# Two-layer cross-attention kernel: the parts of the score maxima and the row normalizations move from VectorE to GpSimd, and the key loads from ScalarE's queue to SyncE's

## The chip, the cores and the metric

One core of one Trainium2 chip. The metric is the device time of one execution in microseconds. The kernel before takes 761.01 us, the median of 3 runs (759.99 to 761.21).

## The reference

`x` is 16 batches of 112 rows of 256 features; the context is 16 batches of 375 rows of 256. Two layers follow each other.

```
x = x + xattn0(layernorm(x), ctx, ctx, mask)      # one head, masked, with a norm of its output
x = x + ffn0(layernorm(x))                        # mixture of experts: 8 routed (2 used per row), 2 shared
x = x + xattn1(layernorm(x), ctx, ctx)            # 16 heads of 16 features, no mask
x = x + ffn1(layernorm(x))                        # x @ W.T + b + (x @ V_r) @ C.T

xattn1: q, k, v = heads of queries @ Wq.T, keys @ Wk.T, values @ Wv.T
        attn = softmax(q @ k.T / sqrt(16)) ; out = (attn @ v) @ Wo.T
layernorm(x) = (x - mean) / sqrt(var + 1e-5)
```

Everything is in float32. The change touches the third line and the normalizations ahead of the third and fourth.

## The kernel before

The first layer and the experts take the time up to about 540 us. The second layer's loop runs over the batches b = 0 to 14, with the two batches ahead begun before it and the last batch behind it (`tensor`, `vector`, `scalar`, `gpsimd` and `sync` of `second_layer` each hold their own copy of that order). All orders are written out by hand, and engines meet only at semaphores. Four batches are a group i (b // 4).

**Scores twice.** The softmax needs the maximum of each row of scores. TensorE multiplies queries and keys once for the maxima (`scores(b, g)`, two heads at a time, g = 0 to 7, line 2134), and VectorE reads the two banks (`maximum(b, g)`, line 1769). The exponentials need the scores the other way round, keys on the partitions, with the maximum taken off. For this queries and keys have rows of their own under the real ones: bf16 parts of a float32 value in three rows each (96 rows are real, `DEPTH`), then three rows that hold the maximum split into three bf16 parts on the queries' side (`qst`), and a constant under the keys (`kst`). `transposed(b, q, ks)` (line 2154) multiplies all 128 rows, so that the maximum is subtracted inside the product. ScalarE takes the exponential (`exps`, line 1981), and TensorE multiplies by the values (`outputs(b, q)`, line 2163), turns the outputs (`outputs_T`, line 2172), and VectorE divides by the sums (`finish(b)`, lines 1794 and 1796, "the heads").

**How the maxima get there.** After `maximum(b, 7)`, `negated_parts(b)` splits the maxima in four small VectorE steps (lines 1776 to 1782). TensorE turns the 48 columns over (`maxima_T(b)`, line 2139), VectorE copies them (`turned(b)`, line 1788), and SyncE sends them as three small transfers to the three rows under the queries (`maxima(b)`, line 1620, "the rows of maxima"). TensorE waits for them ahead of `transposed(b, 0)`.

**The batches overlap.** In iteration b, TensorE makes the scores of batch b + 2, turns the maxima of b + 1, and does the exponentials' products and the outputs of b. Scores use two pairs of banks in turn (`PAIR`, `EARLIER`): a product may start when the one before it in that pair was read. The turned outputs, and the blocks below, take places in that same sequence.

**Blocks.** Between them lie pieces of other stages for a group of four batches: `("q", 3)` in b = 5 (queries of the last group), `("o", i)` in b = 6, 10 and 13 (output projection and addition, `attended`), `("f", i)` in b = 8, 12 and in the tail (the last linear layer, `results`). Each needs normalized rows, apart from "o": `NORMALIZED` puts the statistics (`mean_var`, lines 1719 to 1726) and the normalization (`normalized`, line 1732) of "q" 3 in b = 4 and of "f" 0, 1 and 2 in b = 7, 11 and 14, both on VectorE. GpSimd makes the reciprocal root between them (`rstd_of`, lines 1657 and 1659), adds the last bias (`add_bias`, line 1653), gathers the experts' rows of the last group (`gather`, line 1668), sums them (`combine`, line 1691), and splits queries into bf16 parts (`split_queries`, `split_rest`, lines 1595 to 1603).

**Loads.** The keys of batch b + 4 (three transfers of 378 KB, `load_keys`, line 1571) are asked for on ScalarE's queue at the end of iteration b, after its last exponential. The values of batch b + 1 go the same way for b up to 8 (408 KB). The split queries of a group are stored and loaded again on ScalarE's queue (`store_queries`, `load_queries`).

Of the kernel before, what the change touches and what calls it, by code (L numbers as in the profile page):

```python
# [15 lines left out]
P = 128  # L16
B, S, D = 16, 112, 256
K = 375
# [21 lines left out]
TWO_ONES = 1.0 + 0x3F80 / 2.0 ** 23  # L40
# [1429 lines left out]
def second_layer(nc, tensors, first, routed, dram, out, x_res, weight1, weight2, slots, mhalf, ps, bank, ident, new_semaphore, pool_semaphore):  # L1470
# [111 lines left out]
    def ones_below(pool, b):  # L1582
        pool.memset(kst[b][DEPTH:P, :, :].rearrange("p h t -> p (h t)").bitcast(F32), TWO_ONES).then_inc(s["ones_ready"], 1)
        pool.wait_ge(s["ones_ready"], b + 1)
# [14 lines left out]
    def split_rest(eng, i):  # L1599
        eng.wait_ge(s["q2_ready"], 3 * i + 2)  # L1600
        eng.tensor_copy(qa[:, 2, :, :], qr[:]).then_inc(s["q2_ready"], 1)
        eng.wait_ge(s["q2_ready"], 3 * i + 3)
        eng.tensor_tensor(qa[:, 0, :, :], qr[:], qa[:, 2, :, :], ALU.subtract).then_inc(s["q3_ready"], 1)
        eng.wait_ge(s["q3_ready"], i + 1)

# [4 lines left out]
    def sync(sp):  # L1610
        def load_values(b):
            sp.dma_start(vt[:, b % 2, :, :, :].rearrange("p c h d -> p (c h d)"), vscr[b]).then_inc(s[f"v_in{b % 2}"], 16)

        def maxima(b):
            i, j = divmod(b, G)
            sp.wait_ge(s["mT_ready"], b + 1)

            sp.wait_ge(s["below_ready"], min(i, 1) + 1)
            for k in range(3):
                sp.dma_start(qst[i % 2][DEPTH + k:DEPTH + k + 1, :, j * S:(j + 1) * S], mT[k * NH:(k + 1) * NH, b % 2, :]).then_inc(s[f"mrow_in{b % 2}"], 16)  # L1620

        def results(i):
            for j in range(G):
                sp.wait_ge(s["res_ready"], i * G + (j + 1))
                sp.dma_start(out[i * G + j], x_res[:, i * G + j, :]).then_inc(s["res_out"], 16)


        sp.wait_ge(routed["w2_ready"], NTILE)
        load_keys(sp, 1)
        load_context(sp, NV + 1)  # L1630
        load_context(sp, NV + 2)
        load_values(0)
        for b in range(NV, NV + 3):
            sp.wait_ge(s["v_ps"], b + 1)
            load_context(sp, b + 3)
        maxima(0)
        load_values(1)

        for b in range(B):
            if b + 1 < B:  # L1640
                maxima(b + 1)
            what, i = blocks_in(b)
            if what == "f":
                results(i)
        results(NG - 1)
        sp.wait_ge(s["res_out"], 16 * B)
# [8 lines left out]
    def rstd_of(pool, n, norm, js=slice(0, G)):  # L1655
# [3 lines left out]
        pool.tensor_tensor(rstd[:, js], rstd[:, js], mhalf[:, js], ALU.pow).then_inc(s["rstd_ready"], 1)  # L1659

# [22 lines left out]
    def gpsimd(pool, n):  # L1683

        def combine(i):
            for j in range(G):
# [16 lines left out]
        for j in range(G):  # L1703
            pool.wait_ge(s["p_ready"], (2 * j + 2) * NKC)
            gather(pool, i, j)
        combine(i)
        rstd_of(pool, n, NORMS["q", i])
        split_queries(pool, i)
        split_rest(pool, i)
        for i in range(NG - 1):  # L1710
            rstd_of(pool, n, NORMS["f", i])
            add_bias(pool, i)
# [4 lines left out]
    def mean_var(v, n, i, js=slice(0, G)):  # L1717
        for j in range(js.start, js.stop):
            v.bn_stats(stat[:, j, :], x_res[:, i * G + j, :]).then_inc(s["dve"], 1)
            n()  # L1720
        for j in range(js.start, js.stop):
# [41 lines left out]
    def vector(v, n):  # L1763
        V, done = nc.vector, s["dve"]

        def maximum(b, g):
            v.wait_ge(s["s_ps"], b * 8 + (g + 1))
            p = 2 * PAIR["score", b, g]
            V.tensor_reduce(mxh[:, 2 * g:2 * g + 2], ps[0:S, p:p + 2, 0:K], axis=AX_X, op=ALU.max).then_inc(s["s_max"], 1)  # L1769

        def negated_parts(b):
            base, slot = b * 4, b % 2
            v.wait_ge(s["s_max"], b * 8 + 8)
            if b >= 2:
                v.wait_ge(s["mT_ps"], b - 1)
            V.tensor_scalar(mparts[:, slot, 0, :], mxh[:], -1.0, None, ALU.mult).then_inc(s["m_ready"], 1)
            v.wait_ge(s["m_ready"], base + 1)
            V.scalar_tensor_tensor(mr[:, slot, :], mxh[:], -1.0, mparts[:, slot, 0, :], ALU.mult, ALU.subtract).then_inc(s["m_ready"], 1)
            v.wait_ge(s["m_ready"], base + 2)
            V.tensor_copy(mparts[:, slot, 1, :], mr[:, slot, :]).then_inc(s["m_ready"], 1)  # L1780
            v.wait_ge(s["m_ready"], base + 3)
            V.tensor_tensor(mparts[:, slot, 2, :], mr[:, slot, :], mparts[:, slot, 1, :], ALU.subtract).then_inc(s["m_ready"], 1)
# [50 lines left out]
        negated_parts(0)  # L1833
# [3 lines left out]
        negated_parts(1)  # L1837
# [4 lines left out]
        for b in range(B - 1):  # L1842
# [7 lines left out]
            if kind == "f":  # L1850
                v.wait_ge(s["x3_ready"], k * G + G)
                mean_var(v, n, k)
            elif kind == "q":
# [7 lines left out]
            if kind is not None:  # L1861
                normalized(v, k, NORMS[kind, k])
# [3 lines left out]
            if what == "o":  # L1866
                attended(i)
            elif what == "f":
                results(i)
            if ahead_of:  # L1870
                maximum(b + 2, 7)
                negated_parts(b + 2)
# [73 lines left out]
    def scalar(a):  # L1946
# [59 lines left out]
        for b in range(B - 1):  # L2006
# [7 lines left out]
            if b == G + 2:  # L2014
                store_queries(a, NG - 1)
# [17 lines left out]
            if b + 4 < B:  # L2033
                load_keys(a, b + 4)
# [322 lines left out]
def build_program(nc, dram, outs):  # L2357
    with ExitStack() as ctx, ExitStack() as semaphores:
# [30 lines left out]
        with ExitStack() as lent:  # L2389
# [5 lines left out]
                ("heads", [S, B, D], F32), ("xhL", [P, C, GS], F32), ("mxh", [S, NH], F32), ("mr", [S, 2, NH], F32),  # L2395
# [88 lines left out]
```

## Time and profile before

| | |
|---|---|
| median of 3 runs | 761.01 us |
| profiled execution: its own time | 762.61 us |
| its span | 760.8 us |
| TensorE busy | 732.4 us (96%) |
| VectorE busy | 479.4 us (63%) |
| ScalarE busy | 311.0 us (41%) |
| GpSimd busy | 243.0 us (32%) |
| granted TensorE clock, mean | 0.991 |

The busy shares are of the whole span. The span is the time from the first to the last instruction of the profiled execution; its own time is a little longer. In the rows of stretches, each row is a stretch from one turn of the maxima (line 2139) to the next, so b=3 is 593.75:602.89, b=4, 5, 6 and 7 follow it, and the last two are b=10 and b=11. In the rows, PE is TensorE's products, PEld its loading of weights, DVE VectorE, ACT ScalarE, POOL GpSimd, SP SyncE, and a trailing q is an engine's queue that issues transfers. "[0.94 <-DVE mxh L1769]" behind a row says that the engine was idle for 0.94 us before it, and what ended that.

### The profile page before, as it was taken

Reading aid. Unit: us, or ns where it says so; the run is one execution under the profiler, and the core shown is the slowest. Engines: PE = TensorE matmul, PEld = TensorE weight load, DVE = VectorE, ACT = ScalarE, POOL = GpSimd, SP = SyncE. Lnnn points to the kernel's source line nnn. Section 1 sums busy time; section 2 is a strip of 40 time slices with the busy share of each in tenths; the row PEclk is TensorE's granted clock in tenths of the full one; section 3 lists DMA queues with packets and bytes.
Section 4 is the critical chain, followed back from the end, with each engine's and each line's share of the span. In section 5 each row is a group of like instructions: output and inputs, shape, how many; then the busy total and the mean of one; then the engine's idle time right before and its main releaser. Section 6 shows DMA issues by size and latency. Waiting matters only on the chain.

```text
span 760.8 us, 15546 instructions
## 1 busy us (share of the span) xinstructions
PE 732.4 (96%) x5784; PEld 564.9 (74%) x5784; DVE 479.4 (63%) x1122; ACT 311.0 (41%) x556; POOL 243.0 (32%) x250
## 2 busy tenths in 40 slices
PE   7899999999999999999999999999999998999996
PEld 4576667776776676589999998989777766676775
DVE  4468665356727667824444564838678978888745
ACT  1223211241124122245554555554246764565561
POOL 3775712371151242601301414223743211102021
PEclk9998999999999999999999999999999999999999
DMA  9499932542250296912443423354987765654101
GB/s 257 120 273 326 261 115 83 184 143 82 81 165 13 66 368 249 315 42 69 124 130 102 132 66 99 119 148 125 252 225 207 203 160 170 171 137 125 28 3 49
DMA packets 73068, 113.87 MB, mean 150 GB/s; under 512 B 14929, under 2 KB 59346, under 8 KB 71074
## 3 DMA queue, kind: packets, MB, share of 16 engines
q1 hardware_dynamic: 59200, 66.24, 29.5%
q10 hardware_dynamic: 7634, 30.97, 14.9%
q0 software_dynamic: 6160, 15.67, 6.5%
q8 instruction: 47, 0.77, 0.4%
q14 instruction: 27, 0.22, 0.1%
HBM read 84.27 MB, written 28.41 MB: 148 GB/s over the span
## 4 chain that ended last, share of the span: by engine, by line
PE 79%; DVE 9%; DMA 5%; POOL 3%; issue 1%; ACT 1%; ACTq 0%; SPq 0%; DVEq 0%; POOLq 0%
PE ps L1439 16%; PE ps L1074 12%; PE ps L1448 8%; PE ps L1089 7%; DVE mxh L1769 4%; PE ps L1108 4%; PE ps L2134 4%; PE ps L2163 4%; DMA mask_i<-in_mask 3%; PE ps L2154 3%; PE ps L2127 2%; PE ps L1120 2%; PE ps L1044 2%; PE ps L1016 2%; PE ps L2108 2%; PE ps L2063 2%
## 5 line engine op out<-in xcount | busy, mean ns | idle before, releaser
L1439 PE MATMUL ps<-rowsT,w 128*128 128x128 f32 x1120 | 130.8, 275 | 0.0
L1439 PEld LDWEIGHTS ps<-rowsT,w 128*128 128x128 f32 x1120 | 128.0, 192 | 0.1
L1769 DVE TENSOR_REDUCE mxh<-ps 112x2 f32<-112x750 f32 x128 | 115.0, 931 | 20.1 <-PE ps L2134 18.7
L1981 ACT ACTIVATE d_pT<-ps 125x448 f32<-125x448 f32 x192 | 92.8, 548 | 67.0 <-PE ps L2154 63.5
L1074 PE MATMUL ps<-x1T,sw 128*128 128x448 f32 x256 | 101.3, 540 | 0.0
L1393 ACT ACTIVATE w<-rw 128x1024 f32 x70 | 73.8, 1056 | 59.4 <-PE ps L1439 57.0
L1074 PEld LDWEIGHTS ps<-x1T,sw 128*128 128x128 f32 x256 | 47.5, 190 | 38.8 <-issue 35.9
L2134 PE MATMUL ps<-kst,qst 96*112 96x375 bf16 x256 | 63.8, 336 | 5.9 <-DVE mxh L1769 3.0
L1332 POOL DMA_DIRECT2D yscr<-y x35 | 19.7, 562 | 154.1 <-DVE y L1366 154.1
L1448 PE MATMUL ps<-rw,h 128*128 x280 | 66.4, 380 | 0.0
L884 ACT ACTIVATE silu<-ps,sb 128x448 f32<-128x448 f32 x32 | 20.3, 635 | 98.4 <-PE ps L1074 98.4
L1089 PE MATMUL ps<-sw,gluT 128*112 128x256 f32 x256 | 57.8, 379 | 0.0
L2154 PE MATMUL ps<-qst,kst 128*128 128x112 bf16 x768 | 55.4, 213 | 0.8 <-DMA qst<-mT 0.5
L1448 PEld LDWEIGHTS ps<-rw,h 128*128 128x128 f32 x280 | 50.7, 190 | 6.8 <-issue 1.4
L2154 PEld LDWEIGHTS ps<-qst,kst 128*128 128x128 bf16 x768 | 47.0, 98 | 11.4 <-DMA qst<-mT 1.1
L1089 PEld LDWEIGHTS ps<-sw,gluT 128*112 128x112 f32 x256 | 44.8, 177 | 10.5 <-issue 0.4
L1351 DVE TENSOR_TENSOR h<-ps,rb 128x512 f32<-128x512 f32 x35 | 24.1, 689 | 37.6 <-PE ps L1439 37.6
L341 POOL DMA_INDIRECT xg<-xh_moe,places x32 | 32.5, 1016 | 46.7 <-PE ps L1074 21.9
L1355 DVE TENSOR_TENSOR h<-ps,rb 128x512 f32<-128x512 f32 x35 | 24.2, 691 | 32.5 <-PE ps L1439 32.5
L1668 POOL DMA_INDIRECT yg<-yscr,slots x32 | 31.1, 971 | 25.3 <-ACT d_pT L1981 16.8
L500 DVE SCALAR_TENSOR_TENSOR gluT<-ps,sb,silu 128x448 f32<-128x448 f32 x32 | 21.8, 681 | 26.9 <-ACT silu L884 26.5
L2134 PEld LDWEIGHTS ps<-kst,qst 96*112 96x112 bf16 x256 | 24.2, 129 | 19.6 <-issue 9.4
(248 smaller groups left out, 1188.2 us busy)
## 6 DMA issues: line engine op xcount, KB each, us to landing
kst<-kscr ACTq DMA_DIRECT2D x45, 378.0 KB, 5.2
rw<-in_rw SPq DMA_DIRECT2D x24, 512.0 KB, 9.9
kscr<-ka SPq DMA_DIRECT2D x16, 567.0 KB, 4.1
cT<-in_ctx_t SPq DMA_DIRECT2D x17, 378.0 KB, 5.0
ctxT<-in_ctx_t SPq DMA_DIRECT2D x16, 378.0 KB
ctxn<-in_ctx SPq DMA_DIRECT2D x16, 336.0 KB
qst<-qscr ACTq DMA_DIRECT2D x12, 448.0 KB, 6.5
rows<-xg SPq DMA_DIRECT2D x35, 128.0 KB, 2.7
```

The costliest lines, as they stand in the source:

```text
L341: pool.indirect_dma_start(out=dram["xg"], out_offset=bass.IndirectOffsetOnAxis(ap=places[0:S, k, b:b + 1], axis=0), in_=xh_moe[:, b, :], i ...
L1074: last = mm(bank[up_in(i, m)[k]][:, 0:GS], (sw1, sw2)[k][:, e, c, h * P:(h + 1) * P], x1T[:, c, :], start=c == 0, stop=c == C - 1)
L1089: last = mm(bank[down_in(i, j)][0:S, 0:D], gluT[:, m, j * S:(j + 1) * S], sw3[:, e, h, :], start=m == 0, stop=m == U - 1)
L1108: last = mm(ps[:, 2 + m, 0:KP], wk1[:, c, m * P:(m + 1) * P], context_T(b)[:, c, :], start=c == 0, stop=c == C - 1)
L1393: A(w12[:, k, :, :], (rw1, rw2)[k][:, e, :, :], ACT.Copy).then_inc(s[("w1_ready", "w2_ready")[k]], 1)
L1439: last = mm(bank[1 + 2 * q + k][:, block], w12[:, k, c, block], rowsT[:, q, c * P:(c + 1) * P], start=c == 0, stop=c == C - 1)
L1448: last = mm(y_bank(n)[:, 0:D], h2[:, q, m * P:(m + 1) * P], rw3[:, e, m, :], start=m == 0, stop=m == HM - 1)
L1668: pool.indirect_dma_start(out=yg[:, j, k, :], out_offset=None, in_=yscr[0:DONE[i] * P, :], in_offset=bass.IndirectOffsetOnAxis(ap=slots[0: ...
L1769: V.tensor_reduce(mxh[:, 2 * g:2 * g + 2], ps[0:S, p:p + 2, 0:K], axis=AX_X, op=ALU.max).then_inc(s["s_max"], 1)
L1981: A(pT[:, q % 2, k, :], bank[4 + k][0:KC, 0:QUAD * S], ACT.Exp).then_inc(s["p_ready"], 1)
L2134: last = mm(pair_bank(("score", b, g), k)[0:S, 0:K], qst[i % 2][0:DEPTH, h, j * S:(j + 1) * S], kst[b % 4][0:DEPTH, h, 0:K], start=True, s ...
L2154: last = mm(bank[4 + k][:, h * S:(h + 1) * S], kst[b % 4][:, QUAD * q + h, k * KC:k * KC + P], qst[i % 2][:, QUAD * q + h, j * S:(j + 1) * ...
```

## The change

VectorE's `negated_parts` becomes `parted`, and for batches 2 to 15 GpSimd runs it; the parts are now of the maximum itself and the constant under the keys is minus one instead of one. The maxima have two slots, so that the maxima of one batch can be read while those of the next are written. `normalized_beside` lets GpSimd normalize the rows of "q" 3 and of "f" 0, 1 and 2. VectorE makes the statistics of "f" in the "o" block itself (b = 6, 10, 13): two rows' between the additions, the others after maximum 7. The statistics of "q" 3 stay in b = 4. SyncE asks for the keys of batch b + 4, after the rows of maxima of b + 1 and a wait for the last product of `transposed(b, 3)`. `store_queries` of the last group moves from the start of b = 6 to its end.

```diff
-TWO_ONES = 1.0 + 0x3F80 / 2.0 ** 23
+TWO_MINUS_ONES = -1.0 - 0xBF80 / 2.0 ** 23
...
+    def parted(eng, b):
+        base, slot = b * 4, b % 2
+        eng.wait_ge(s["s_max"], b * 8 + 8)
+        if b >= 2:
+            eng.wait_ge(s["mT_ps"], b - 1)
+        eng.tensor_copy(mparts[:, slot, 0, :], mxh[:, slot, :]).then_inc(s["m_ready"], 1)
+        eng.wait_ge(s["m_ready"], base + 1)
+        eng.tensor_tensor(mr[:, slot, :], mxh[:, slot, :], mparts[:, slot, 0, :], ALU.subtract).then_inc(s["m_ready"], 1)
+        eng.wait_ge(s["m_ready"], base + 2)
+        eng.tensor_copy(mparts[:, slot, 1, :], mr[:, slot, :]).then_inc(s["m_ready"], 1)
+        eng.wait_ge(s["m_ready"], base + 3)
+        eng.tensor_tensor(mparts[:, slot, 2, :], mr[:, slot, :], mparts[:, slot, 1, :], ALU.subtract).then_inc(s["m_ready"], 1)
...
     # sync, loop over b
             if what == "f":
                 results(i)
+            if b + 4 < B:
+                sp.wait_ge(s["st_ps"], (b + 1) * 4 * NKC)
+                load_keys(sp, b + 4)
...
+    def normalized_beside(pool, i, norm):
+        pool.wait_ge(s["rstd_ready"], MV + norm + 1)
+        for j in range(G):
+            pool.tensor_scalar(xh[:, j, :], x_res[:, i * G + j, :], mv[:, j, 0:1], rstd[:, j:j + 1],
+                               ALU.subtract, ALU.mult).then_inc(s["xh_ready"], 1)
...
     # gpsimd
         for j in range(G):
+            if j % 2:
+                parted(pool, j // 2 + 2)
             pool.wait_ge(s["p_ready"], (2 * j + 2) * NKC)
             gather(pool, i, j)
-        combine(i)
+        for j in range(0, G, 2):
+            combine(i, range(j, j + 2))
+            parted(pool, j // 2 + 4)
         rstd_of(pool, n, NORMS["q", i])
+        normalized_beside(pool, i, NORMS["q", i])
+        parted(pool, 6)
+        parted(pool, 7)
         split_queries(pool, i)
         split_rest(pool, i)
-        for i in range(NG - 1):
+        for i, batches in enumerate(((8,), (9, 10, 11, 12), (13, 14, 15))):
+            for b in batches:
+                parted(pool, b)
             rstd_of(pool, n, NORMS["f", i])
+            normalized_beside(pool, i, NORMS["f", i])
             add_bias(pool, i)
...
     # vector
         def maximum(b, g):
+            if g == 0 and b >= 2:
+                v.wait_ge(s["m_ready"], (b - 2) * 4 + 2)
...
     # vector, loop over b
             turned(b + 1)
-            if kind == "f":
-                v.wait_ge(s["x3_ready"], k * G + G)
-                mean_var(v, n, k)
-            elif kind == "q":
+            if kind == "q":
                 v.wait_ge(s["added"], 2 * G)
                 mean_var(v, n, k)
             if b:
                 finish(b - 1)
...
-            if kind is not None:
-                normalized(v, k, NORMS[kind, k])
...
             if what == "o":
-                attended(i)
+                attended(i, slice(0, 2))
+                v.wait_ge(s["x3_ready"], i * G + 2)
+                row_stats(v, n, i, slice(0, 2))
+                attended(i, slice(2, G))
             elif what == "f":
                 results(i)
             if ahead_of:
                 maximum(b + 2, 7)
-                negated_parts(b + 2)
+            if what == "o":
+                v.wait_ge(s["x3_ready"], i * G + G)
+                row_stats(v, n, i, slice(2, G))
+                rows_joined(v, n)
...
     # scalar, loop over b
             exps(b, 0, range(2, NKC))
-            if b == G + 2:
-                store_queries(a, NG - 1)
             exps(b, 1)
...
             exps(b, 3, range(1, NKC))
-            if b + 4 < B:
-                load_keys(a, b + 4)
+            if b == G + 2:
+                store_queries(a, NG - 1)
```

## Rows read from the trace of the kernel before

**Rows 1.** Busy by stretch: us, PE, PEld, DVE, ACT, POOL, clock, DMA share, GB/s.
```profile
593.75:602.89 9.14, 9.14 (x167) 6.77 (x165) 8.49 (x16) 7.63 (x18) 2.92 (x4) 1.00 0.68 182
602.89:614.15 11.26, 9.54 (x167) 6.76 (x165) 11.09 (x28) 6.17 (x14) 1.28 (x2) 1.00 1.02 258
614.15:628.40 14.25, 13.21 (x183) 9.07 (x182) 9.81 (x15) 8.34 (x18) 3.87 (x4) 1.00 0.53 135
628.40:642.89 14.49, 13.82 (x189) 10.38 (x189) 11.09 (x21) 6.82 (x15) 1.80 (x1) 1.00 0.47 144
642.89:654.39 11.50, 9.53 (x168) 6.84 (x166) 11.18 (x28) 6.18 (x14) 4.05 (x6) 1.00 0.60 167
...
677.52:691.21 13.69, 13.57 (x191) 10.36 (x189) 10.09 (x20) 7.14 (x16) 0.00 (x0) 1.00 0.33 86
691.21:702.46 11.25, 9.52 (x167) 6.85 (x166) 11.08 (x28) 6.18 (x14) 4.04 (x6) 1.00 0.51 128
```

**Rows 2.** Waits from 550 us on: total us, times, longest.
```profile
ACT d_pT L1981 <- POOL qa L1603: 3.0, 1, 3.0
PE ps L2134 <- DVE mxh L1769: 3.0, 4, 0.9
PE ps L2134 <- DVE heads L1796: 2.6, 3, 1.0
PEld ps L2154 <- DMA qst<-mT: 1.1, 2, 0.9
```

**Rows 3.** Timeline of b=7, VectorE and TensorE: start, duration, instruction.
```profile
643.62 1.41 DVE L1719 BATCH_NORM_STATS2 d_stat<-x_res 112x6 f32<-112x256 f32 x4 [0.15 <-issue]
...
645.96 0.53 PE L2134 MATMUL ps<-kst,qst 96*112 96x375 bf16 x2 [1.04 <-DVE heads L1796]
...
648.36 1.37 DVE L1732 TENSOR_SCALAR d_xh<-x_res,d_mv,d_rstd 112x256 f32<-112x256 f32 x4
...
650.63 0.53 PE L2134 MATMUL ps<-kst,qst 96*112 96x375 bf16 x2 [0.94 <-DVE mxh L1769]
```

**Rows 4.** Timeline of the end of b=5.
```profile
625.31 1.89 POOL L1597 TENSOR_TENSOR qr<-qr,qa 128x896 f32<-128x896 f32 x1
625.39 1.84 DVE L1778 SCALAR_TENSOR_TENSOR mr<-mxh,mparts 112x16 f32<-112x16 f32 x1
...
627.26 0.17 DVE L1780 CAST mparts<-mr 112x16 bf16<-112x16 f32 x1
...
628.40 0.21 PE L2139 MATMUL ps<-identb,mparts 112*48 112x112 bf16 x1 [0.93 <-DVE mparts L1782]
```

**Rows 5.** Timeline of a plain stretch, b=2 to b=3.
```profile
589.85 1.77 DVE L1769 TENSOR_REDUCE mxh<-ps 112x2 f32<-112x750 f32 x2
...
592.84 0.34 ACTq L1988 DMA_DIRECT2D vt<-vscr  x1
...
593.75 0.23 PE L2139 MATMUL ps<-identb,mparts 112*48 112x112 bf16 x1
...
594.34 2.74 SPq L1620 DMA_DIRECT2D qst<-mT  x3
...
600.50 0.55 PEld L2154 LDWEIGHTS ps<-qst,kst 128*128 128x128 bf16 x8
```

**Rows 6.** Groups of GpSimd's instructions by line: busy us, mean ns.
```profile
L296 POOL TENSOR_SCALAR keep<-mask_i 112x375 f32<-112x375 int32 x16 | 24.6, 1538 | 28.0 <-DVE nmx L443 17.7 <-DMA mask_i<-in_mask 10.1
...
L1657 POOL TENSOR_SCALAR d_rstd<-d_mv 112x4 f32<-112x4 f32 x7 | 1.6, 231 | 93.6 <-DVE d_mv L1726 93.6
...
L1659 POOL TENSOR_TENSOR d_rstd<-d_rstd,mhalf 112x1 f32<-112x1 f32 x1 | 0.6, 567 | 0.1
```

**Rows 7.** Transfers from 560 us on: KB each, median us to landing.
```profile
kst<-kscr ACTq DMA_DIRECT2D x38, 378.0 KB, 5.2
vt<-vscr ACTq DMA_DIRECT2D x8, 408.0 KB, 6.1
```

**Rows 8.** Landing of the rows of maxima, whole second layer.
```profile
DMA to landing us min/median/max: 1.7/3.8/7.6
```

More of the change, by code:

```diff
@@ L1582, in ones_below @@
     def ones_below(pool, b):
-        pool.memset(kst[b][DEPTH:P, :, :].rearrange("p h t -> p (h t)").bitcast(F32), TWO_ONES).then_inc(s["ones_ready"], 1)
+        pool.memset(kst[b][DEPTH:P, :, :].rearrange("p h t -> p (h t)").bitcast(F32), TWO_MINUS_ONES).then_inc(s["ones_ready"], 1)
         pool.wait_ge(s["ones_ready"], b + 1)
@@ L1683, in gpsimd, with combine @@
     def gpsimd(pool, n):
-        def combine(i):
-            for j in range(G):
+        def combine(i, js):
+            for j in js:
                 for k in range(2):
@@ L1715, in gpsimd, with row_stats @@
         rstd_of(pool, n, NORMS["f", i] + 1, LAST)
-    def mean_var(v, n, i, js=slice(0, G)):
+    def row_stats(v, n, i, js=slice(0, G)):
         for j in range(js.start, js.stop):
@@ L1720, in mean_var, with rows_joined @@
             n()
+    def mean_var(v, n, i, js=slice(0, G)):
+        row_stats(v, n, i, js)
+        rows_joined(v, n, js)
+    def rows_joined(v, n, js=slice(0, G)):
         for j in range(js.start, js.stop):
@@ L1766, in maximum @@
         def maximum(b, g):
+            if g == 0 and b >= 2:
+                v.wait_ge(s["m_ready"], (b - 2) * 4 + 2)
             v.wait_ge(s["s_ps"], b * 8 + (g + 1))
             p = 2 * PAIR["score", b, g]
[L1769 to L1782, printed above, removed]
+            V.tensor_reduce(mxh[:, b % 2, 2 * g:2 * g + 2], ps[0:S, p:p + 2, 0:K], axis=AX_X, op=ALU.max).then_inc(s["s_max"], 1)
         def turned(b):
@@ L1832, in vector @@
             maximum(0, g)
-        negated_parts(0)
+        parted(v, 0)
         turned(0)
@@ L1836, in vector @@
             maximum(1, g)
-        negated_parts(1)
+        parted(v, 1)
         v.wait_ge(s["v_ready"], B)
@@ L2394, in build_program @@
                 ("d_pT", [KC, 2, NKC, GS], F32), ("outT", [P, 4, S], F32),
-                ("heads", [S, B, D], F32), ("xhL", [P, C, GS], F32), ("mxh", [S, NH], F32), ("mr", [S, 2, NH], F32),
+                ("heads", [S, B, D], F32), ("xhL", [P, C, GS], F32), ("mxh", [S, 2, NH], F32), ("mr", [S, 2, NH], F32),
                 ("mparts", [S, 2, 3, NH], BF16), ("mT", [3 * NH, 2, S], BF16), ("rec", [S, NH], F32)))
```

## The prediction, made before the change was run

> **What bounds the kernel now.** The change touches only the second layer's attention, from about 565 us on, so I read that part alone. I number the stretches by the loop's batch b, and cut them where TensorE turns the maxima of the next batch over. First view: busy time by stretch [rows 1]. A stretch with nothing but attention takes 9.14 us and TensorE is busy all of it (b=3: 9.14 of 9.14); one with a block ("q", "o" or "f") takes 13.69 us (b=10). Those two are TensorE's own pace, and nothing that the other engines save there can count. Four kinds of stretch stand above the pace: b=4 by 2.12 us (11.26), b=7 by 2.36 (11.50), b=11 by 2.11 (11.25), and b=5 and b=6, which I come back to. In b=4, 7 and 11 VectorE is busy for 11.1 to 11.2 us of 11.25 to 11.5, against 8.5 us in a plain stretch: these are the three batches in which it makes row statistics and normalizes rows while scores are still to be read.
>
> Second view: TensorE's waits [rows 2]. Scores wait 2.6 us three times for the heads and 3.0 us four times for maxima, all told. Third view: the order of time in b=7 [rows 3]. The statistics (1.41 us) stand ahead of the heads, and TensorE waits for these and starts score 3 after 1.04 us of idleness. The four normalizations (1.37 us) stand ahead of maximum 5, and TensorE idles another 0.94 us. So the price of rows work on VectorE is about 1 us for each of the two places, in each of three stretches. In b=14 the same work costs nothing: there are no more scores ahead, and the last 32 us (tail) go by exponentials and products.
>
> Fourth view: the end of b=5 [rows 4]. VectorE's second step of the parts took 1.84 us instead of 0.17, and ended with GpSimd's subtraction of the queries (625.31 + 1.89). TensorE then waited 0.93 us to turn the maxima over, and stretch b=6 is 14.49, 0.80 above its pace. That accident costs 0.93 + 0.80 = 1.73 us.
>
> **The change, part by part.**
>
> *Parts on GpSimd.* Four VectorE steps per batch go for batches 2 to 15, and GpSimd does them. Budget: in a plain stretch the last maximum ends at 589.85 + 1.77 = 591.62 and TensorE wants the parts at 593.75 [rows 5], so 2.13 us. GpSimd has no such instruction before the change. Nearest rows [rows 6]: a scalar operation on 4 columns 0.23 us, a power of one column 0.57. Lower bound for a step: VectorE's 0.17 us (the cast in [rows 4]); upper bound that 0.57. I take 0.25: these are 16 columns, nearest to the 4-column row. With about 0.1 us between steps (each waits for the one before) and at the ends the chain is 4 x 0.25 + 0.4 = 1.4 us: hidden by the score products and exponentials, with 0.7 us to spare. At 0.57 for the two subtractions and 0.3 for the two copies it is 2.1 us: just at the edge. Cost 0 in stretches; if the cover went, each 0.1 us beyond 2.13 would cost 0.1 us in each of 13 stretches. Only in b=13, where no scores stand between, is the gap shorter: 0 to 0.5 us late, I take 0.1.
>
> What stands in GpSimd's queue around it: parts of 2 and 3 stand ahead of two gathers, which then start about 1.7 us later. Their rows are scaled a batch later, so nobody waits. In b=2 and 3 the parts follow the sums of the gathered rows, whose last ends within 0.2 us of the last maximum. Parts of 7 now stand ahead of the query split and not beside it: the accident of b=5 and 6 goes, gain 1.7 us.
>
> In plain stretches VectorE gets back about 0.8 us, worth nothing: TensorE is already busy throughout.
>
> *Two slots of maxima.* The new wait of a batch's first maximum is for parts made a whole stretch earlier: 0.
>
> *Normalizing on GpSimd.* Nearest row: a two-operation scalar instruction on 375 columns, 1.54 us [rows 6]; by column this is 1.05 us for 256. Lower bound VectorE's 0.34 (1.37 / 4, [rows 3]), upper 1.54; I take 1.05, so 4.2 us for four. For "q" 3 they end near 611 and are wanted in b=5; for "f" 0 and 1 they start a stretch earlier than now and are wanted a stretch later. For "f" 2 they end about 735 where TensorE wants them about 736; at 1.54 each this would be 0.7 us late. So 0, and up to 0.7 for the range. It takes the normalizations out of VectorE in b=4, 7, 11: the second gap of each (0.94 us in b=7) goes.
>
> *Statistics moved to the "o" blocks (b=6, 10, 13).* Two of four go between the additions, while VectorE waits for products anyway (free). The other two and the joining (0.7 + 0.4 us) come after maximum 7, where the parts (0.8 us) have left. So VectorE enters b=7 and b=11 some 0.4 us later than now. Walking its queue: maximum 1 then ends about 0.2 us after TensorE wants that pair of banks; the heads end just in time. I take a new gap of 0.2 us (bounds 0 and 0.6). Net gain b=7: 2.36 - 0.2 = 2.15; b=11: 2.11 - 0.2 = 1.9. In b=13 it is beside TensorE's last score-free part: 0.
>
> *b=4.* Here ("q" 3) the statistics stay ahead of the heads, so the first gap of 1 us stays; only the second goes, at most 2.12 - 1.04 = 1.08 us. But TensorE met another wait right behind: about 0.2 us for the row of maxima (the shorter of two such waits, 1.1 us together and the longer, in b=1, 0.9 [rows 2]). Arriving 0.9 us earlier it finds the row 0.9 us farther away, unless it lands earlier. So the gain is 0 to 1.08; I take 0.7, as the row's landing moves a little with the earlier gathering of traffic.
>
> *Keys asked for by SyncE.* The request waits for the same product as the exponential that now stands ahead of it on ScalarE, so it starts at the same moment. ScalarE loses three issues (about 0.6 us each) per batch, in which its next exponential was not yet due: 0. But the transfers move to SyncE's queue, in front of the rows of maxima. Keys take 5.2 us to land, values 6.1 [rows 7], rows of maxima 3.8 in the median, 1.7 at best and 7.6 at worst [rows 8]. In a plain stretch values are asked for at 592.8 [rows 5] and all in flight has landed by 592.8 + 6.1 = 598.9; a row queued behind everything would then land some 1.7 us later, 600.6, and TensorE wants it at 600.5 [rows 5]. So even the full queue costs 0.1 us a stretch. I take 0.3 us over all for b=1, 2 and 9, bounds -0.5 and +2.
>
> The Trainium skill, "DMA: Bandwidth & Descriptors", section on queues, rings and completion order, says that an issuing engine has one ring on each DMA engine, consumed in order, and that a semaphore's increment lands only after every earlier write of that engine, across its queues. By the second half a row of maxima waits for the keys in either arrangement, and the move is worth 0; by the first half alone it would be the slower rival below. The 3.8 us in the median for so small a transfer, against 1.7 at best, agree with the second half.
>
> *The store of queries* moves from b=6's start to its end. ScalarE waited 3.0 us there for GpSimd [rows 2], which is part of the accident above; now the split ends near 632 and the store comes near 640: 0.
>
> *VectorE held up by GpSimd.* The stall in [rows 4] could return elsewhere, as GpSimd works more. What stays on VectorE in the loop reads either banks or one tile. The Trainium skill, "SBUF — State Buffer", on who interferes with whom, says that a VectorE instruction with two SBUF inputs is held by a GpSimd one that reads SBUF, one with a single input outside the two-port modes is not. The trace agrees: the 1.84 us step has two such inputs. By it the new order is free of the stall.
>
> Sum: 1.7 (b=5, 6) + 2.15 (b=7) + 1.9 (b=11) + 0.7 (b=4) - 0.1 (b=13) - 0.3 (rows of maxima) = 6.05 us. The profiled execution has a span of 760.8 us and took 762.61; the median is 761.01. I take the sum from the median: 755.0 us.
>
> **Rivals.**
> 1. *All stalls go.* The row of maxima lands early enough in b=4, and no new gap opens after "o": 1.7 + 2.36 + 2.11 + 1.08, and 0.5 us of the DMA wait in b=1: 7.8 us, 753.2; with b=4's first gap too, 752.2. For it: VectorE has 0.8 us more air everywhere. Against: b=4's statistics stay where they were.
> 2. *Half is given back.* Statistics after maximum 7 are late by 0.6 us in b=7 and 11, and b=4 gains nothing, f 2 comes 0.7 late, rows of maxima cost 1 us: 6.05 - 0.8 - 0.7 - 0.7 - 0.7 = 3.15, 757.9.
> 3. *Slower: rows of maxima behind keys.* If SyncE's queue delays each row by L, b=1 and b=4 lose all L (they wait already), and b=2, 3, 7 and 9 lose L less their slack (asked for at 594.3 and wanted at 600.5 [rows 5], 6.2 us, less 1.2 for three issues and 3.8 to land, so 1.2). It turns the gain at 2L + 4(L - 1.2) = 6, so L = 1.8 us; with L = 4 it loses 19.2, net 13 slower: 774. For it: DMA is busy up to all of the time in b=4 (share 1.02, [rows 1]). Against: the bound above, since the keys must land anyway.
> 4. *GpSimd's parts too slow.* Above 0.5 us a step the chain passes 2.13 us; at 1 us it takes 4.4 - 2.1 = 2.3 us in 13 stretches, 30 us: 785. Against: the power of one column, the slowest for its size, takes 0.57 [rows 6].
>
> **How the numbers follow.** Less than 0.2% (1.5 us) cannot be told from no change. Forecast 0.60 (own range 753 to 757.5), rival 1 0.12, rival 2 0.14, rival 3 0.11 (of which 0.06 within 0.2%, since an L near 1.8 just cancels), rival 4 0.03. Rivals 3 and 4 give slower 0.08 together; same 0.08, with a little of rival 2; faster 0.84. Range 752 to 759.5: it takes in rivals 1 and 2 and the bounds of the terms.
>
> **What would show it.** After: stretches like b=7 and b=11 near 9.3 us and b=4 near 10.4; b=5 and 6 without the wait for parts; GpSimd's four steps ending before the turn; steps of about 0.25 us, normalizations about 1.05; no row of maxima waited for by more than 1 us. Wrong if: TensorE waits for the row of maxima in most stretches, or for GpSimd's parts, or if plain stretches differ from 9.14 us, on which nothing here says that they can change.

## The result, and the profile after

The changed kernel takes 758.12 us (median of 12 runs, 754.61 to 761.41), the kernel before beside it 762.23 us (12 runs, 758.41 to 766.46). The ratio is 0.9926, 95% interval 0.9902 to 0.995; by it, from the 762.23, the gain is 5.6 us (interval 3.8 to 7.5); the two medians differ by 4.1. The forecast was 755.0 from 761.01, a ratio of 0.9921 and a gain of 6.05. A second series of 12 gave 757.74 us and a ratio of 0.9943 (0.9916 to 0.997), a gain of 4.3 (2.3 to 6.4). So both series show a gain, and its size is uncertain by some 2 us.

The profiled execution of after is a long one: span 759.6 us, own time 761.40. Its second layer begins late. The turn of the maxima in b=0 starts at 570.56 us, in the kernel before at 565.16, and in the other traces of this study anywhere from 561.09 to 571.81. That is ahead of everything that the change touches, so the spans say little here. I compare the 14 stretches from that turn to the turn of b=14: 164.00 us before, 157.40 after, 159.06 in a second trace of the changed kernel. Gains of 6.60 and 4.94 us, 5.8 in the mean. What follows b=14's turn is 31.64 us in both profiles.

Busy time by stretch of the changed kernel, same columns as [rows 1]; b=3, 4, 5, 6, 7, then b=10 and 11:

```profile
598.31:607.46 9.15, 9.15 (x167) 6.78 (x166) 7.93 (x12) 7.75 (x18) 3.69 (x8) 1.00 0.69 186
607.46:618.33 10.87, 9.52 (x168) 6.74 (x166) 9.31 (x20) 6.17 (x14) 6.91 (x10) 1.00 1.01 267
618.33:631.58 13.25, 13.13 (x183) 9.04 (x181) 8.12 (x12) 8.24 (x18) 1.88 (x6) 1.00 0.47 127
631.58:645.27 13.69, 13.57 (x192) 10.36 (x190) 10.98 (x24) 7.26 (x16) 6.21 (x9) 1.00 0.48 120
645.27:655.37 10.10, 9.32 (x168) 6.71 (x166) 7.98 (x12) 6.18 (x14) 8.77 (x13) 1.00 0.89 247
...
678.30:691.99 13.69, 13.57 (x192) 10.35 (x190) 10.98 (x24) 7.26 (x16) 1.74 (x6) 1.00 0.32 89
691.99:701.27 9.28, 9.22 (x168) 6.82 (x166) 8.11 (x12) 6.31 (x14) 8.72 (x13) 1.00 0.48 123
```

The plain stretch and the block are where they were (9.15, 13.69): TensorE's own pace. b=11 has come down to it, b=4 has hardly moved, b=7 has come a little more than halfway. b=6 lies on the pace of a block. b=5 is at 13.25, which every trace repeats that has neither the accident nor another load in this stretch, so the "q" block's own pace is 13.25 and not the 13.69 of the others. VectorE's 11.1 us of b=4, 7 and 11 are 9.3, 8.0 and 8.1.

The waits of the changed kernel from 550 us on, as in [rows 2]:

```profile
PEld ps L2183 <- DMA qst<-mT: 2.4, 4, 1.1
PE ps L2183 <- DMA qst<-mT: 1.3, 2, 0.8
PEld ps L2163 <- DVE heads L1826: 1.0, 1, 1.0
PE ps L2163 <- DVE heads L1826: 0.8, 1, 0.8
```

Products waited 5.6 us for VectorE's maxima and heads before [rows 2]; now it is 0.8, once, in b=4. In exchange they wait 1.3 us, in two waits, for the rows of maxima (before: 0.52 us once, in b=1). Both, in order of time (b=4, b=7):

```profile
616.08 0.57 PE L2183 MATMUL ps<-qst,kst 128*128 128x112 bf16 x8 [0.56 <-DMA qst<-mT]
653.12 0.57 PE L2183 MATMUL ps<-qst,kst 128*128 128x112 bf16 x8 [0.78 <-DMA qst<-mT]
```

GpSimd's new instructions, first the first two steps of the parts (counts, shortest/median/longest ns), then the timeline in b=13 and 14 with the normalizations:

```profile
L1612 POOL CAST mparts<-mxh x14: 190/196/197, 577.9 to 726.6; 112x16 bf16<-112x16 f32 x14
L1614 POOL TENSOR_TENSOR mr<-mxh,mparts x14: 217/218/223, 578.2 to 726.9; 112x16 f32<-112x16 f32 x14
```

```profile
726.58 0.20 POOL L1612 CAST mparts<-mxh 112x16 bf16<-112x16 f32 x1 [12.64 <-DVE mxh L1812]
...
727.41 0.22 POOL L1618 TENSOR_TENSOR mparts<-mr,mparts 112x16 bf16<-112x16 f32 x1
...
729.06 4.83 POOL L1683 TENSOR_SCALAR d_xh<-x_res,d_mv,d_rstd 112x256 f32<-112x256 f32 x4
```

A step takes 0.20 to 0.22 us (forecast 0.25) and the four 1.05 us from first start to last end (726.58 to 727.63, and the same to 0.02 elsewhere); four normalizations take 4.83 us (forecast 4.2), and end at 733.89, 1.20 us ahead of the first product that reads them (735.09). In b=2 the parts end at 597.32, 0.99 us ahead of the turn. The normalizations of "q" 3 end at 616.03 and not near 611 as forecast, and the parts of batch 6, which stand behind them, 1.28 us ahead of their turn. TensorE never waits for either.

### The profile page after: what moved, and what is told of

Same layout as the page of the kernel before. It is cut to its first block, busy times and chain, and to the rows that moved or that the text cites. A ratio compares the mean times of both kernels' runs of the same rounds, so it can differ in the third digit from the quotient of the medians.

```text
span 759.6 us, 15555 instructions
## 1 busy us (share of the span) xinstructions
PE 731.1 (96%) x5784; PEld 563.2 (74%) x5784; DVE 465.4 (61%) x1050; ACT 311.8 (41%) x556; POOL 273.6 (36%) x322
## 4 chain that ended last, share of the span: by engine, by line
PE 83%; DMA 7%; DVE 4%; SPq 3%; issue 1%; POOL 1%; ACT 1%; ACTq 0%; DVEq 0%; POOLq 0%
PE ps L1439 15%; PE ps L1074 12%; PE ps L1089 7%; PE ps L1448 7%; PE ps L2163 5%; PE ps L2192 5%; PE ps L1108 5%; PE ps L2183 4%; PE ps L1120 3%; PE ps L2156 2%; PE ps L1044 2%; PE ps L2137 2%; DMA mask_i<-in_mask 2%; PE ps L1051 2%; DMA qst<-mT 2%; PE ps L2092 2%
## 5 line engine op out<-in xcount | busy, mean ns | idle before, releaser
L1074 PE MATMUL ps<-x1T,sw 128*128 128x448 f32 x256 | 103.0, 547 | 0.0
```

The source lines that it names most:

```text
L1074: last = mm(bank[up_in(i, m)[k]][:, 0:GS], (sw1, sw2)[k][:, e, c, h * P:(h + 1) * P], x1T[:, c, :], start=c == 0, stop=c == C - 1)
```

## The experiments

All start from the changed kernel but one. "Stretch" is as above, the "sum" is that of the 14 stretches; each value is from one trace unless said. Experiments 1 to 8 and 11 have one run each, and its time says little: the turn in b=0, ahead of everything that was edited, is spread over 10.7 us.

| | sum of the 14 stretches, us | own time of the profiled run, us |
|---|---|---|
| before | 164.00 | 762.61 |
| changed, and once more (12) | 157.40, 159.06 | 761.40, 756.69 |
| 1 keys on ScalarE | 157.65 | 753.81 |
| 2 store in the middle | 156.74 | 762.00 |
| 3 store at the start | 162.79 | 761.98 |
| 4 statistics of "q" 3 early | 161.87 | 762.51 |
| 5 parts on VectorE | 162.66 | 759.17 |
| 6 normalizations on VectorE | 159.31 | 754.88 |
| 7 statistics of "f" ahead of the heads | 158.97 | 759.63 |
| 8 queries' load in b=5 | 156.92 | 751.45 |
| 9 both transfers moved | 157.29 | 756.67 |
| 10 the three moves | 155.53 | 755.73 |
| 11 kernel before, two orders | 162.60 | 760.89 |

The two traces of the changed kernel lie 1.66 us apart, so sums are told apart only beyond about that; single stretches without a transfer repeat to a few hundredths.

**1. Keys asked for by ScalarE again.**

```diff
-                sp.wait_ge(s["st_ps"], (b + 1) * 4 * NKC)
-                load_keys(sp, b + 4)
...
     # scalar, end of the loop, behind store_queries
+            if b + 4 < B:
+                load_keys(a, b + 4)
```

> The changed kernel, with the keys of batch b + 4 asked for on ScalarE's queue again; all else of the change stays. In the changed kernel TensorE waits for the row of maxima 0.78 us in b=7 (stretch 10.10 us) and 0.56 us in b=4 (10.87). Theory A (the rows of maxima now queue behind the keys on SyncE's queue): the wait in b=7 goes, the stretch falls to about 9.3 us, and rows of maxima land in 3.7 us or so as before, so this part of the change cost 0.8 us or more. Theory B (the cause is the store of the queries, 672 KB, now asked for at the end of b=6 and in flight in b=7; the queue of the keys does not matter): b=7 stays near 10.1 us and b=4 near 10.9.

```profile
599.79:610.85 11.06, 9.52 (x167) 6.74 (x166) 9.31 (x20) 6.17 (x14) 6.91 (x10) 1.00 1.02 264
610.85:624.10 13.25, 13.13 (x183) 9.05 (x181) 8.12 (x12) 8.07 (x18) 1.88 (x6) 1.00 0.48 126
624.10:638.65 14.55, 14.00 (x191) 10.39 (x189) 11.48 (x24) 6.98 (x16) 6.97 (x10) 1.00 0.52 150
638.65:647.80 9.15, 9.15 (x166) 6.78 (x166) 7.58 (x11) 6.17 (x14) 8.03 (x12) 1.00 0.73 194
```

b=4 to b=7. The wait in b=7 is gone, as A says, but b=6 has lost as much (14.55 against 13.69): ScalarE's queue now issues the store and three key loads one after the other, from 634.28 to 637.14, and its next exponential starts at 637.18 after 2.36 us of idleness; TensorE waits 0.31 us for it, and is busy for 14.00 us of the stretch instead of 13.57. In b=7 the rows of maxima land in 4.4 to 4.9 us (5.2 to 6.0 in the changed kernel), but the store is also asked for 4.9 us ahead of them instead of 4.1, so this run alone does not tell A from B. The sum, 157.65 us, lies between the two traces of the changed kernel. So the queue of the keys is worth nothing that these traces can tell, on this path; what it does is keep ScalarE's queue clear where the store stands.

**2. Store in the middle of b=6.**

```diff
             exps(b, 2, range(1, NKC))
+            if b == G + 2:
+                store_queries(a, NG - 1)
             scaled(b, 2)
...
             exps(b, 3, range(1, NKC))
-            if b == G + 2:
-                store_queries(a, NG - 1)
```

> The changed kernel, with the store of the last group's queries moved from the end of b=6 to its middle, behind the exponentials of the third quarter, some 5 us earlier. Theory A (queue of the keys): b=7 stays at about 10.1 us with a wait of 0.8 us for the row of maxima. Theory B (the store's traffic): the wait shrinks or goes, b=7 falls to between 9.3 and 9.6 us; b=6 stays at 13.69, since the queries' parts are ready by then.

```profile
646.73:656.08 9.35, 9.22 (x168) 6.82 (x166) 8.18 (x12) 6.38 (x15) 8.79 (x13) 1.00 0.64 182
```

b=7 is 9.35 us against 10.10, with the keys still on SyncE's queue, and b=6 is 13.69. The rows of maxima land in 3.5 to 4.2 us there instead of 5.2 to 6.0. Theory B: the wait in b=7 was the store's traffic. Two more kernels with the store in this place gave 9.34 and 9.34; all seven traces with it at the end and keys on SyncE gave 9.93 to 10.26 (in three of them, experiments 5 to 7, TensorE comes later for VectorE's sake and waits for that instead).

**3. Store back at the start of b=6**, ahead of `exps(b, 1)`, as before the change.

> The changed kernel, with the store of the queries back at the start of b=6, where ScalarE must wait for GpSimd's split, which ends some 2 us into b=6. Theory A (moving the store was needed, its wait stalls the exponentials and by them TensorE): b=6 grows from 13.69 us by 0.5 to 2 us, and what this costs is part of the 1.8 us that b=5 and b=6 gained together. Theory B (ScalarE has air enough there, all of the gain in b=5 and b=6 came from VectorE's step no longer being held up): b=6 stays within 0.1 us of 13.69. By either, if the store's traffic makes b=7's wait, b=7 falls to about 9.3 us.

ScalarE waits 4.9 us for GpSimd's split, TensorE 3.23 us for ScalarE. b=6 takes 19.38 us, 5.69 more, far above A's bound. Windows over that place:

```profile
626.00:629.70 3.70, 3.70 (x63) 2.46 (x51) 2.79 (x6) 1.41 (x3) 3.56 (x4) 1.00 0.96 258
629.70:632.94 3.24, 0.01 (x1) 0.00 (x1) 0.94 (x1) 0.60 (x2) 2.11 (x2) 0.83 0.52 124
632.94:636.00 3.06, 3.06 (x19) 2.40 (x20) 0.00 (x0) 2.32 (x6) 0.00 (x0) 0.50 0.61 221
636.00:639.00 3.00, 3.00 (x38) 2.25 (x38) 1.78 (x2) 0.92 (x4) 0.00 (x0) 0.56 0.00 0
```

After 3.24 us with nothing to do, TensorE's granted clock is 0.50 (1.2 of 2.4 GHz) for the next 3 us and 0.56 in the 3 behind them; eight products of `transposed` take 0.99 us there, where they take 0.56 to 0.65 at a clock of 1.00. b=7 is 9.35 here as well. So the move of the store, which I priced at nothing, was needed once the parts of 7 stand ahead of the split.

**4. Statistics of "q" 3 at the end of b=3.**

```diff
-            if kind == "q":
-                v.wait_ge(s["added"], 2 * G)
-                mean_var(v, n, k)
...
+            elif b == G - 1:
+                v.wait_ge(s["added"], 4)
+                row_stats(v, n, NG - 1, slice(0, 2))
             if ahead_of:
                 maximum(b + 2, 7)
+            if b == G - 1:
+                v.wait_ge(s["added"], 2 * G)
+                row_stats(v, n, NG - 1, slice(2, G))
+                rows_joined(v, n)
```

> The changed kernel, with the statistics of the last group's query rows made at the end of b=3 (two rows ahead of maximum 7, two and the joining behind it) and no longer ahead of the heads of b=4. Theory A (the 0.79 us gap of TensorE in b=4 is VectorE's statistics alone): that gap goes, but the row of maxima lands no earlier, so TensorE meets it 0.8 us sooner and waits for it longer: b=4 stays between 10.5 and 10.9 us. Theory B (the gap and the row's landing are one chain, since everything asked for in b=4 follows TensorE): b=4 falls by 0.8 us to about 10.1. b=3 stays at 9.15 (within 0.3).

```profile
615.64 0.93 PE L2187 MATMUL ps<-qst,kst 128*128 128x112 bf16 x8 [3.46 <-DMA qst<-mT]
```

The gap for the heads goes and b=4 takes 14.61 us, which neither theory held. TensorE now waits 3.46 us for the row of maxima, which took 5.4 to 8.4 us to land (4.2 to 6.8 in the changed kernel, up to 7.4 in experiments 3, 5, 6 and 7), and then runs eight products in 0.93 us instead of 0.57, at a granted clock of 0.50 from 615.64 to 618.04. Coming early is no gain in front of a late transfer, and can be a loss. Why the rows landed 1.0 to 1.6 us later than elsewhere is not shown; it is one trace.

**5. Parts on VectorE again**: `parted(v, b + 2)` behind `maximum(b + 2, 7)`, GpSimd's calls gone.

> The changed kernel, with the parts of the maxima of batches 2 to 15 on VectorE again, behind maximum 7; statistics, normalizations, two slots and loads stay as changed. Theory A (moving the parts paid only by taking VectorE's two-tile steps out of the way of GpSimd, which now also normalizes rows): plain stretches stay at 9.15 us, b=5 is 13.25 to 14.3, and wherever GpSimd sums or normalizes at the end of a stretch the steps grow from 0.17 us up to 1.2 us each. Theory B (the four steps, 0.8 us, also counted in the stretches behind an o block, where statistics stand on them): b=7 and b=11 grow by 0.3 to 0.9 us over 10.1 and 9.3. By A alone b=11 stays within 0.1 us of 9.3.

```profile
622.72 1.89 POOL L1597 TENSOR_TENSOR qr<-qr,qa 128x896 f32<-128x896 f32 x1
622.80 1.84 DVE L1614 TENSOR_TENSOR mr<-mxh,mparts 112x16 f32<-112x16 f32 x1
...
625.81 0.21 PE L2162 MATMUL ps<-identb,mparts 112*48 112x112 bf16 x1 [0.94 <-DVE mparts L1618]
```

The accident of [rows 4] is back to the hundredth: b=5 14.25, b=6 15.98, more than in the kernel before since the granted clock fell, to 0.50 from 628 to 629 and 0.68 from 629 to 632. TensorE's two gaps there are those of the kernel before (0.94 and 0.55 us, before 0.93 and 0.55). b=11 is 9.73 (+0.45): in its first gap, 0.31 us, TensorE waits for a maximum that stands behind the parts and the statistics on VectorE, as B says. b=7 has the same gap of 0.31 us but stays at 9.98, since its wait for the row of maxima took it in. b=12 is 14.27 (+0.60), and this is A: beside GpSimd's additions of the last bias (694.84 to 697.62) the first two steps take 0.62 and 0.65 us instead of 0.17. The first of them is a copy with a single input. The sum, 162.66 us, is 4.4 above the mean of the changed kernel, more than in experiments 6 (1.1) and 7 (0.7); but 3.3 of it is the accident in b=5 and b=6, which experiment 11 undoes without moving work between engines.

**6. Normalizations on VectorE again**, ahead of maximum 5 as before.

> The changed kernel, with the normalizations of q 3 and f 0, 1, 2 on VectorE again (ahead of maximum 5 in b=4, 7, 11, 14); statistics stay in b=6, 10, 13. Theory A (the 1.4 us of VectorE ahead of maximum 5 are what opened the second gap of 0.94 us): b=11 grows from 9.28 to about 10.0 us (VectorE's new air of 0.8 us takes a part of the 1.4), b=7 too unless its wait for the row of maxima takes it in. Theory B (with parts and statistics gone from the stretch VectorE has air enough, and the normalizations could have stayed): b=11 stays within 0.15 us of 9.28.

```profile
684.47:694.73 10.26, 9.32 (x167) 6.80 (x166) 9.18 (x16) 6.17 (x14) 3.87 (x9) 1.00 0.55 142
```

b=11 takes 10.26 us, 0.98 more, all of the second gap; VectorE's new air takes in none of it. A, with a larger size. b=7 is 10.26 and b=4 11.53.

**7. Statistics of "f" ahead of the heads again** (b=7, 11, 14). GpSimd makes the parts of batches 9 and 13 behind the normalizations, not ahead of them.

> The changed kernel, with the statistics of f 0, 1, 2 back ahead of the heads in b=7, 11, 14; GpSimd makes the parts of 9 and 13 between the normalizations and the bias so that these do not wait. Theory A (the first gap of 1.04 us is the statistics ahead of the heads): b=11 grows by 0.9 to 1.1 us to about 10.3; b=6 and b=10 stay at 13.69, and b=7 grows by less, since its wait for the row of maxima shrinks by what TensorE comes later. Theory B (the gain in b=11 came from the normalizations and parts alone): b=11 stays near 9.3.

```profile
687.85:697.99 10.14, 9.35 (x168) 6.84 (x166) 9.32 (x20) 6.18 (x14) 7.47 (x11) 1.00 0.45 118
```

b=11 takes 10.14 us, 0.86 more, with a gap of 0.79 us for the heads: theory A, a little under its bounds. b=7 stays at 10.14, with the same gap and no wait for the row of maxima any more: the one took the other in. In the tail TensorE waits 1.3 us for GpSimd's normalizations, which this order makes late.

**8. Load of the third group's queries in b=5** instead of b=4.

```diff
-            if b in (G, 2 * G):
+            if b in (G + 1, 2 * G):
                 load_queries(a, b // G + 1)
```

> The changed kernel, with the load of the third group's queries (three transfers of 448 KB) asked for in b=5 and not in b=4; batch 8 needs them in b=6. Theory A (these 1.34 MB are what makes the row of maxima land 6 to 8 us after it is asked for in b=4): the row lands in under 5.5 us, the wait goes, b=4 falls from 10.87 to about 10.2 us (the 0.79 us gap for the heads stays) and b=5 stays at 13.25. Theory B (the keys and values in flight are enough): b=4 stays between 10.7 and 11.1.

b=4 takes 10.13 us against 10.87 and 11.52 in the two traces of the changed kernel: theory A. The rows of maxima of b=4 land in 3.4 to 3.8 us instead of 4.2 to 6.8; those of b=5 now take 5.4 to 7.9 (4.0 to 4.6 in the changed kernel), and there TensorE does not wait for them. b=5 takes 13.43, 0.18 more.

**9. Both transfers moved** (2 and 8).

> The changed kernel with two transfers moved: the store of the last queries to the middle of b=6, the load of the third group's queries to b=5. Theory A (each transfer made one wait for the row of maxima, and they add): b=4 about 10.15 us, b=5 13.25 to 13.45, b=7 9.2 to 9.35, all else as changed; the 14 stretches from b=1 on take about 156.0 us against 157.4. Theory B (traffic moved elsewhere makes its wait elsewhere): the sum stays within 0.4 us of 157.4.

b=4 10.13, b=7 9.34, as A says; b=5 takes 14.59, where A had at most 13.45, with 1.30 us ahead of the first score of batch 8. The profile names no releaser there; the likely one is the load of the queries, which now stands in b=5 and took 7.2 to 9.6 us to land. Experiment 8 has the same load in the same place (6.4 to 8.5 us) and takes only 13.43, experiment 10 13.53: the load now lands barely in time, and whether b=5 pays for it varies between traces. The sum is 157.29, theory B's. Ratio to the kernel before 0.9882 (0.9838 to 0.9925), 4 runs.

**10. The three moves together** (2, 4 and 8).

> As the kernel with two moved transfers, and the statistics of the last group's query rows at the end of b=3. Theory A (with the load gone from b=4 the row of maxima lands in time even when TensorE comes 0.8 us earlier, so that the 3.5 us wait seen with this move alone does not come back): b=4 falls to 9.2 to 9.7 us, the sum of the stretches to about 155.3, the median about 2 us below the changed kernel's. Theory B (the row then lands late all the same, as TensorE meets it sooner): b=4 stays above 10.1 us.

```profile
603.69:613.22 9.53, 9.41 (x167) 6.82 (x165) 8.51 (x13) 6.25 (x14) 6.66 (x9) 1.00 0.67 168
613.22:626.75 13.53, 13.18 (x183) 9.04 (x181) 8.12 (x12) 8.13 (x18) 2.16 (x6) 1.00 0.85 229
```

b=4 takes 9.53 us, DMA share 0.67 instead of 1.01. Theory A: statistics made early pay, once the queries' load is out of the way. The sum is 155.53 us, the lowest of all. Median 756.01 us beside the changed kernel's 757.74, ratio to the kernel before 0.9904 (0.9871 to 0.9937). That lies below the changed kernel's 0.9926 and 0.9943, but the intervals overlap: by the stretches of this one trace it is better than the change by 1.9 to 3.5 us, by the runs not shown. b=5, with the load of the queries in it, is at 13.53, and 1.1 us of the difference from experiment 9 is that stretch's scatter.

**11. The kernel before, with only two orders changed.**

```diff
+        pool.wait_ge(s["m_ready"], 7 * 4 + 4)
         split_queries(pool, i)
```

and the store in the middle of b=6.

> The kernel before, with two orders changed and nothing moved between engines: GpSimd waits for VectorE's parts of batch 7 before it splits the queries, and ScalarE stores them in the middle of b=6. Theory A (the loss in b=5 and b=6 is VectorE's two-tile step held up by GpSimd's subtraction, and nothing else): b=5 falls from 14.25 to 13.25 us and b=6 from 14.49 to about 13.7, b=4, 7 and 11 stay at 11.3 to 11.5. Theory B (part of it is VectorE being too busy with the parts): b=5 or b=6 keep 0.4 us or more of their excess.

```profile
614.51:627.76 13.25, 13.13 (x183) 9.04 (x182) 8.72 (x16) 8.07 (x18) 1.27 (x2) 1.00 0.45 124
627.76:641.45 13.69, 13.57 (x192) 10.37 (x190) 10.09 (x20) 7.12 (x16) 4.39 (x3) 1.00 0.60 170
```

b=5 and b=6 fall to their pace, 1.80 us together, with the parts still on VectorE, whose second step takes 0.178 us at most: an order undoes the accident as well as a move. How much of it was the step held up by GpSimd, and how much ScalarE's wait of 3.0 us for the split [rows 2], this run does not part, since both orders changed. Experiment 5 does for the most part: there the store stands at the end, the stall is back, and with it both gaps, 0.94 and 0.55 us. So 1.5 of the 1.80 us is the step's; the rest, for which TensorE was busy longer in the kernel before (13.82 against 13.57 us in b=6), is not attributed.

**12. The changed kernel once more.**

> The changed kernel itself once more, beside the others on the same chip. All theories: stretches within 0.1 us of those seen (b=4 10.9, b=7 10.1, b=11 9.3) where no transfer is waited for, up to 0.5 us off in b=1, b=4 and b=7, and the median 4 to 7 us below the kernel before.

b=5, 6 and 11 give 13.25, 13.69 and 9.29, the same to a hundredth. Stretches with a wait for a transfer scatter: b=2 9.65 against 9.20, b=4 11.52 against 10.87, b=7 9.98 against 10.10. So does b=8, 14.24 against 13.78, where TensorE waits 0.48 us for ScalarE's copy of the turned rows (`d_xhT`); what made that late is not shown.

## Why the prediction came out right

The mechanism was right for b=5, 6 and 11: their 3.6 us were forecast and 3.8 came. The size of the whole (6.05 us forecast; 5.6 and 4.3 by the ratios of the two series, 5.8 by the stretches) came out near in part by luck. Two terms were set too high, by 1.3 us together (b=7 and b=4); others came out 1.0 us better than forecast, and 0.7 of that is b=1, where the forecast had a small loss. The time itself, 758.12 us, lies in the stated range (752 to 759.5) but above the forecast's own narrower one (753 to 757.5), by the side of rival 2 (757.9); part of this is that the kernel before took 762.23 us beside it and not 761.01. Of rival 2's steps one came true, that b=4 gains nothing, and with it, in b=7, a part of the loss that it gave to the rows of maxima; the gap behind the "o" block was not 0.6 us and "f" 2 was not late. Gains in us; the two values are the two traces of the changed kernel:

| stretch | forecast | measured | |
|---|---|---|---|
| b=5 and 6 | 1.7 | 1.80, 1.80 | right; experiments 5 and 11 show most of the cause |
| b=11 | 1.9 | 1.97, 1.96 | right; 6 and 7 give 0.98 and 0.86 for its two gaps |
| b=7 | 2.15 | 1.40, 1.52 | too high by the store's traffic (experiment 2) |
| b=4 | 0.7 | 0.39, -0.26 | too high: the row of maxima takes it all in |
| b=13 | -0.1 | -0.01, -0.01 | right |
| b=1 | part of -0.3 | 0.69, 0.70 | sign wrong; luck |
| b=2, 8 and 9 | rest of it | 0.15, -0.76 | scatter (the forecast had b=1, 2 and 9) |
| b=0 | 0 | 0.20, -0.01 | |

**Steps that held.** Removing rows work from VectorE gave back both gaps of about 1 us where no transfer is late. The parts on GpSimd fitted, with 1.05 us for four steps (forecast 1.4 with the ends). A normalization took 1.21 us there (forecast 1.05), inside its bounds. The new gap behind an "o" block (forecast 0.2 us) is 9.28 - 9.14 = 0.14 in b=11. Plain stretches did not move where no transfer is waited for. The sum for b=5 and 6 put b=6's excess and b=5's gap together, which was right although a "q" block's pace was read as 13.69 us: b=5 stood 1.00 us above its pace of 13.25, not 0.56. Rival 4's threshold has a slip: with the forecast's own 0.4 us for steps between and ends, four steps pass 2.13 us above 0.43 us each, not 0.5. The stall of VectorE's two-tile steps came back nowhere in the changed kernel.

**"The store of queries moves from b=6's start to its end: 0."** This step failed twice over. The move was worth 5.7 us against not moving it (experiment 3), and its new place cost 0.6 to 0.75 us in b=7 (9.98 and 10.10 against 9.35), as 672 KB are then in flight beside the row of maxima (landing 5.2 to 6.0 us there, 3.6 to 4.4 in the kernel before). Together the move was worth about 5 us. I had asked who waits for the store, and not what its bytes stand beside.

**"I take 0.7" for b=4.** The case was seen (a wait behind the gap) and then priced too kindly. In the six traces with b=4's load, statistics and normalizations as changed (the changed kernel twice, experiments 1, 2, 3 and 7) the stretch takes 10.87 to 11.52 us, 11.2 in the mean, against 11.26 in the kernel before and 11.41 in its reordered form: next to nothing is gained. The queries' load is what holds the row of maxima there; without it b=4 is 10.13, and 9.53 with early statistics.

**Keys on SyncE's queue** (forecast 0, and 0.3 us of loss in b=1, 2 and 9; the slower rival if each row landed 1.8 us later). Experiment 1 puts it at nothing that these traces can tell. In the median the rows of maxima land in 4.1 and 3.6 us in the two traces of the changed kernel, and 3.6 in the kernel before (from 560 us on); but the last two record the landings of every second batch only and miss b=4, so the medians, the 3.8 of [rows 8] among them, say little. The Trainium skill, "DMA: Bandwidth & Descriptors", on queues, rings and completion order, says that a transfer's semaphore increment lands only after every earlier write of the same DMA engine, whichever queue it came by. Experiment 8 agrees: the load that it moves is asked for on ScalarE's queue, and the rows sent by SyncE's queue land in 4.2 to 6.8 us behind it and in 3.4 to 3.8 without it. DMA engines that merely share their time between the queues would give the same, and no run parts the two.

**b=1, which the forecast had with a small loss.** TensorE waited there for the row of maxima, 0.52 us in the kernel before (9.84) and 1.14 in its reordered form (10.45), and no longer waits. With keys on SyncE's queue and gathers as early as before (experiment 5) it takes 9.26 us; with keys on ScalarE's queue and the later gathers that the parts bring (experiment 1) 9.16; with both 9.14 to 9.16. So either of the two is enough for nearly all of it, and which of them does it in the changed kernel cannot be said. Rival 1 had this gain, at 0.5 us, and the forecast did not.

## What to carry to other kernels

Where one engine bounds the kernel, find the pace of a stretch that waits for nothing and count only what others exceed it by; here that named b=5, 6, 7 and 11, which brought 5.2 of the 5.8 us. When a transfer is moved, price its bytes at the new place, and not only its issue and its waiter. A wait removed in front of another wait is worth nothing until that one moves too, and orders alone can undo an accident between two engines.

## What the runs showed of the hardware

- A wait of 3.2 to 3.5 us of TensorE costs 1.6 to 1.8 times its length: 5.69 us for 3.23 (experiment 3), and 14.61 - 9.15 = 5.46 us above the pace for 3.46 (experiment 4, granted clock 0.50 in the 2.4 us behind it). Waits of TensorE of 0.94 and 0.55 us close together brought the clock down once (experiment 5: 0.50 from 628 to 629 us, 0.68 from 629 to 632) and left it at 1.00 in the kernel before.
- A VectorE subtraction of two SBUF tiles of 16 columns that starts 0.08 us behind a GpSimd subtraction ends 0.03 us behind that one's end, 1.84 us instead of 0.17, alike in two kernels (before, experiment 5). A VectorE copy with one SBUF input, 112x16 from float32 to bf16, was held too, 0.62 us instead of 0.17 beside GpSimd's additions of 112x256 (experiment 5, 696.35 us).
- GpSimd takes 0.20 us for a copy and 0.22 for a subtraction of 112x16, VectorE 0.17; on 112x256 a normalization takes 1.21 us on GpSimd and 0.34 on VectorE. Both could be moved without cost here because TensorE came for neither before it was done; the small step is dearer by 0.03 to 0.05 us, the wide one by 0.87.
- Small transfers of 3.5 KB land in 1.7 to 1.8 us where the DMA engines are nearly idle (b=13, share 0.04) and in up to 8.4 us beside a load of 1.34 MB (b=4 of experiment 4, share 0.97).
